# A vision-transformer block in float32: the residual's load is issued one image earlier and moved ahead of the loads of normalised tokens

## The reference

```python
h = _L0_tok_ref(x, L0_tok_W, L0_tok_b)
h = jnp.concatenate([jnp.broadcast_to(cls_tok, (h.shape[0], 1, h.shape[2])), h], axis=1)
h = h + _L0_attn_ref(_layernorm(h, axis=-1), ...)   # softmax(q k' * scale + anchor term) v, times Wo
h = h + _L0_ffn_ref(_layernorm(h, axis=-1), ...)    # round and clip to int8, matmul, scale, bias
return h
```

## Time and profile before

| | |
|---|---|
| median of 3 runs | 1740.1 us (1738.42 to 1743.04) |
| the profiled execution: time, span | 1741.97 us, 1740.2 us |
| attention phase | from about 425 us to the end |
| busy share of the span: PE, DVE, POOL, ACT | 92%, 88%, 61%, 50% |
| length of an odd and an even step together, around 1000 us | about 19.4 us |
| DMA busy share in the attention phase | 0.75 to 0.82 in stretches of 200 us |
| granted TensorE clock in the attention phase | 1.00 of full speed |

### The profile page before, as it was taken

How to read it: one execution, slowest core, us unless ns; L and a number is a source line. 1 busy time by engine, 2 the same in 40 slices (tenths; PEclk the granted TensorE clock), 3 DMA queues, 4 the chain that set the end, 5 groups by cost and what they waited for, 6 DMA issues and landing times.

```text
span 1740.2 us, 52082 instructions
## 1 busy us (share of the span) xinstructions
PE 1607.0 (92%) x15856; PEld 1406.2 (81%) x15856; DVE 1523.9 (88%) x3521; ACT 868.0 (50%) x2008; POOL 1064.6 (61%) x2039
## 2 busy tenths in 40 slices
PE   4999999996699999999999999999999999999995
PEld 4999999995577778888788888878778877878874
DVE  7888888895389899999999999999999999999995
ACT  2000000002266666666666666666666666666663
POOL 3353453535056667676667767676767677676775
PEclk9999999997599999999999999999999999999997
DMA  9998899973677878887888878887888888887851
GB/s 304 273 322 282 316 296 300 323 252 128 113 133 146 147 142 149 145 148 140 143 153 148 146 141 150 145 147 141 147 153 147 144 142 152 145 148 141 148 108 33
DMA packets 216157, 303.64 MB, mean 174 GB/s; under 512 B 47776, under 2 KB 205011, under 8 KB 205988
## 3 DMA queue, kind: packets, MB, share of 16 engines
q1 hardware_dynamic: 204690, 227.17, 66.3%
q10 hardware_dynamic: 7426, 39.47, 7.8%
q0 software_dynamic: 3984, 36.28, 5.4%
HBM read 126.54 MB, written 58.29 MB: 106 GB/s over the span
## 4 chain that ended last, share of the span: by engine, by line
PE 20%; DMA 14%; issue 13%; DVE 13%; SPq 10%; POOL 4%; ACT 2%; DVEq 1%; ACTq 1%; POOLq 0%
DMA h_in<-h_scratch 13%; SPq L766 6%; PE bank L877 5%; DVE neg_max L1184 4%; PE o_bank L933 4%; PE s_pair L911 3%; PE bank L925 2%; DVE x_lo L1248 2%; DVE h L1271 2%; DVE rough L1283 2%; SPq L756 2%; PE bank L898 2%; PE bank L1024 1%; PE bank L1062 1%; SPq L774 1%
## 5 line engine op out<-in xcount | busy, mean ns | idle before, releaser
L1078 ACT ACTIVATE probs<-bank 99x396 f32<-99x396 f32 x768 | 380.3, 495 | 171.9 <-PE bank L925 165.4
L340 PE MATMUL bank<-e_t,xt 128*128 128x192 f32 x2352 | 386.6, 328 | 25.2 <-DVE xt L448 21.5
L340 PEld LDWEIGHTS bank<-e_t,xt 128*128 128x128 f32 x2352 | 385.1, 191 | 26.5 <-DVE xt L448 26.3
L1184 DVE TENSOR_REDUCE neg_max<-s_pair 99x4 f32<-99x788 f32 x384 | 374.1, 974 | 21.1 <-PE s_pair L911 20.9
L1308 POOL TENSOR_TENSOR key_sum<-probs 99x396 f32<-99x396 f32 x256 | 307.8, 1202 | 103.4 <-ACT probs L1078 74.5
L925 PE MATMUL bank<-q_st,k_st 99*99 99x198 f32 x1536 | 297.0, 275 | 5.3 <-ACT probs L1078 4.6
L1346 POOL TENSOR_TENSOR hb<-h,ffn_bias 99x384 f32<-99x384 f32 x128 | 129.1, 1009 | 235.9 <-DVE h L1271 235.9
L925 PEld LDWEIGHTS bank<-q_st,k_st 99*99 99x99 f32 x1536 | 195.8, 166 | 87.6 <-ACT probs L1078 44.5
L911 PE MATMUL s_pair<-k_st,q_st 96*99 96x198 f32 x1536 | 224.4, 269 | 31.7 <-DVE neg_max L1184 30.3
L448 DVE STREAM_TRANSPOSE xt<-x_t 128x256 f32<-128x256 f32 x588 | 215.0, 416 | 43.5 <-PE bank L340 42.1
L933 PE MATMUL o_bank<-probs,vals 99*32 99x198 f32 (+1 forms) x3072 | 224.2, 338 | 0.0
(11 more groups left out here) (137 smaller groups left out, 3703.1 us busy)
## 6 DMA issues: line engine op xcount, KB each, us to landing
x_t<-in_x_dram SPq DMA_DIRECT2D x26, 1344.0 KB, 21.2
x_t<-in_x_dram ACTq DMA_DIRECT2D x26, 1344.0 KB, 22.4
q_st<-qk_hi SPq DMA_DIRECT2D x126, 198.0 KB, 4.3
k_st<-qk_hi SPq DMA_DIRECT2D x126, 198.0 KB, 4.5
xn_in<-xn_scratch SPq DMA_DIRECT2D x128, 148.5 KB
h_in<-h_scratch SPq DMA_DIRECT2D x128, 148.5 KB
h_scratch<-h_t POOLq DMA_DIRECT2D x13, 1344.0 KB, 17.8
xn_scratch<-xn_t POOLq DMA_DIRECT2D x13, 1344.0 KB, 8.1
```

Source lines behind the costliest of these rows:

```text
L340: last = pe.matmul(token_bank(p)[:, 0:D], xt[:, p, c // 3, c % 3, :], e_t[:, row_kind(t), col, c // 3, c % 3, :], start=c == 0, stop=c == 5)
L1078: nc.scalar.activation(probs[:, n.two, h, :, :], wide(T_BANK, TC), ACT.Exp).then_inc(exp_done, 1)
L1184: nc.vector.tensor_reduce(out=neg_max[:, n.two, :, 2 * j:2 * j + 2].rearrange("p c h -> p h c"), in_=both, axis=AX_X, op=ALU.max, negate=T ...
```

## The change

In the step of image i, SP used to issue the residual of image i-2 (`e`), the one that DVE adds in the same step, after the even step's stacks. It now issues the residual of image i-1 (`c`), after the odd step's first two stacks and ahead of `load_xn`. In an even step, which has no stacks at that point, it is the first thing that SP issues. The wait that protects the buffer (`h1_done`, for the image two before) moves with it. Nothing else is changed.

```diff
-                f, p, a, e, k, ahead = i.plus(5), pair_of(i), i.plus(1), i.plus(-2), i.plus(-5), i.plus(7)
+                f, p, a, c, k, ahead = i.plus(5), pair_of(i), i.plus(1), i.plus(-1), i.plus(-5), i.plus(7)
...
                     stack(p, q_st, 0, q_first, qk_hi[:, 0, :])
                     stack(p, q_st, 1, q_first, qk_hi[:, 0, :])
+                if c.within(B):
+                    if c.reuses(NS):
+                        sp.wait_ge(h1_done, c.count(1, 1 - NS))
+                    sp.dma_start(h_in[:, c.two, :, :], h_dram[c.n].rearrange("(c p) d -> p c d", p=TC))\
+                        .then_inc(h_landed[c.slot], 16)
                 if ahead.within(B):
                     load_xn(ahead)
...
                     stack(p, k_st, 1, k_last, qk_lo[:, 2, :])
-                if e.within(B):
-                    if e.reuses(NS):
-                        sp.wait_ge(h1_done, e.count(1, 1 - NS))
-                    sp.dma_start(h_in[:, e.two, :, :], h_dram[e.n].rearrange("(c p) d -> p c d", p=TC))\
-                        .then_inc(h_landed[e.slot], 16)
                 if k.within(B):
```

## The result

The changed kernel takes 1733.96 us (median of 6 runs, 1731.92 to 1739.87) against 1740.2 us before (6 runs). The ratio is 0.9963, with a 95% interval of 0.9948 to 0.9977: faster by about 6 us, where 25 us were forecast, and the time lies inside the stated range of 1703 to 1736 us. The direction was right and the size was not, by a factor of four. A few runs of the whole set were in a slower state (one of e13's six, at 2209.75 us, and three of the kernel before beside e13 to e15), and all ratios leave them out.

What follows compares the result with a forecast made beforehand. A late residual load was taken to stall DVE, and through it PE, once per pair of steps. 28 us regained less 3 us for the stacks gave 25 us: 1715 us against the median, range 1703 to 1736 us.

Steps and rivals of the forecast that it cites:

- The stall that goes: At L1271 DVE no longer waits for the residual; PE gets back its L911 wait for `neg_max`, 28 us.
- What is next at L1271: The output projection is next in line, 0.09 us ahead of DVE, so DVE regains 0.5 of 0.57 us.
- The wait for the buffer: The new load's wait for `h1` of the image two before is met by 0.6 us or more; cost 0.
- The even step, 3 us: Residual ahead of three stacks shifts the last by 0.55 us; mean cost 0.05 us over 61 pairs, 3 us.
- upper bound of 1.1 us: Largest shift of the even step's last stack, if SP's issue and the queue's transfer are both paid.
- the first rival: Shorter odd step makes even-step stacks 1.0 us later; 15 of 28 us given back at L911, 1727 us; chance 0.20.
- The slack: Last stack's landing to the first score's weights: 0.85 us in the typical pair, 0.45 in another, next to nothing in a slow one.
- a pair of 18.9 to 19.1 us: Sign in the profile after: the length of a pair of steps if the forecast is right.
- its second or fourth case: Stacks give part back (0.20) or make it slower (0.08); sign: L911 or `qk_hi` waits for `k_st` of 10 us or more.
- the slower one: Last stack gates every pair before the first score; each 0.3 us longer, 18 us, 1758 us; chance 0.08.
- The odd step, 0 us: The load changes places with two token loads; the same bytes stand before the seven stacks, cost 0.
- The stores, 0: The stores keep their place in both steps, so no cost was put on them.

Runs made afterwards that it cites:

- e13: As e11, with the large load of the normalised tokens cut in two halves too: 1727.8 us, ratio 0.9926.
- e15: Changed kernel with the large load of the normalised tokens, not the residual, cut in two halves: 1719.05 us, ratio 0.988.
- e1: Changed kernel, image ahead kept, but the residual's load issued at its old place behind the even step's three stacks: 1714.95 us, ratio 0.9864.
- e5: Changed kernel with the residual at the new place in odd steps only, at the old place in even steps: 1718.69 us, ratio 0.9875.
- e6: Changed kernel with the residual at the new place in even steps only, at the old place in odd steps: 1725.49 us, ratio 0.9915.
- e10: Changed kernel with the residual's load cut by token chunk into two halves, both at the new place: 1721.19 us, ratio 0.9888.
- e11: As e1, with the residual's load cut by token chunk into two halves, both at the old place: 1706.63 us, ratio 0.9798.
- e3: As e1, with the even step's loads of normalised tokens behind the three stacks too: 1731.08 us, ratio 0.9951.

## Why the prediction was wrong

**The stall that goes: right.** 28 us were to come from PE's wait for `neg_max`. The wait is gone, and where nothing takes its place, in e1, the kernel gains 24 us by its medians (1738.6 to 1714.95).

**What is next at L1271: right.** The output projection, 2.0 us in two waits.

**The wait for the buffer: right.** No wait of SP at L792 appears in the trace after between 500 and 1700 us; SP waits for `mrow_done` and `qkhi_done` as before, for the latter longer (42.8 us against 27.7), which fits ACT's rewriting of `qk_hi` being late.

**The even step, 3 us: the step that failed.** The place, the mechanism and the releaser were right, and the size was nearly eight times too small: 23.5 us of waits at L911 in place of 3, and 19 us of time (the changed kernel against e1). The mis-sized term is the shift of the last stack. The prediction took 0.55 us, since issue and transfer "overlap rather than add". Against SP's row maxima, the measure that it had named itself, the stack now lands 1.11 us later on average: it is issued 0.50 us later and takes 0.60 us longer to land (table above). That is the prediction's upper bound of 1.1 us, but its second half has another source. In e1 the landing is 0.54 us longer too, with the residual behind the stacks. So it is not the transfer of the residual ahead of the stacks. It goes with the shorter odd step, 8.84 us in place of 9.30 from its first stack to the row maxima, which is the 0.46 us that the forecast left out and the first rival put on top. What the place adds is SP's issue time, 0.5 us, near the 0.58 us that the prediction had read as a bound. The idle 0.6 us of the earlier trace rows hid neither.

The slack was read rightly. In the trace before, the time from the last stack's landing to the first score's weights is 0.71 us on average over 61 pairs. By these slacks a shift of 0.55 us in every pair gives 2.2 us of waits, close to the 3 us of the sum, and one of 1.1 us gives 24, close to the 23.5 measured. The second figure is an estimate: the real shift is uneven, and the pair after the loop's turn pays most of it.

The first rival, 1.0 us of shift and 1727 us, was therefore nearest, and the 1733.96 us lie in the band that it was given (1724 to 1735). The time is inside the stated range by that rival and not by the forecast. The signs say the same: the prediction asked for a pair of 18.9 to 19.1 us, and the trace after has 19.52 against 19.58 before, where e1 has 19.11; and it said that 10 us or more of waits for `k_st` would prove its second or fourth case, the first rival or the slower one.

**The odd step, 0 us: wrong.** e5 and e6 put 4 to 8 us on it. The same bytes stand before the seven stacks, but the load now comes before the tokens. How that slows the stacks behind both is open.

**The stores, 0: not contradicted**; nothing was run on them.

**The rule of the Trainium skill** ("DMA: Bandwidth & Descriptors", section "Queues, rings and completion order"), that an increment lands only after the engine's earlier writes, would show here as a longer time from a stack's issue to its landing when the residual is ahead of it. No run shows that apart: 5.92 us in the changed kernel against 5.85 in e1, and 5.14 in e10 against 5.33 in e11. Nor does it cover e3, where 9.3 KB were late through what was issued behind them, or the cut: no run here shows why one DMA of two chunks holds the queue longer than two DMAs of one chunk.

**Still open:** whether it is the number of partitions, the two chunks or the pauses between two issues that makes the cut loads cheaper; why the landing lengthens in the pair after the loop's turn and not in the others as much; and what the bytes ahead would cost if their issue took SP no time.

## What to carry to other kernels

Before a load is moved forward in a queue, find the transfer behind it with the least slack and add up everything that makes it later: the time that the issuing engine needs for the load (0.5 us here), and what goes with the gain of the change itself, here a longer landing (0.5 to 0.6 us). Each alone fits into a slack of 0.7 us in most pairs, and both together do not. Issuing early and issuing ahead are two changes: take the earlier image at the old place first (here 24 us against 6). When a DMA queue is nearly full, the form of a transfer is worth a try by itself, and only together with the wait that it relieves: the same cut gave 8 to 13 us where the stacks were late or nearly so, nothing where DVE's stall set the pace, and a loss of 21 us where one more was added.

## What the runs showed of the hardware that was not expected

The same 148.5 KB over 99 partitions, in two DMAs of 74 KB in place of one, let the 99 KB transfers issued after it land in 2.9 us instead of 3.6 us, and cutting the tokens' load of the same shape did as much for the time. The small transfer of 9.3 KB (`q_st<-max_rows`) was late 39 times, 22.4 us in all, when the large transfers behind it were issued right after it, and 12 times, 4.6 us, when two loads stood between them. A 198 KB transfer within on-chip memory took 5.0 us or 6.97 us to land in neighbouring pairs of the same loop; the long landing recurred in one pair of three (17 of 20 over 6.2 us), with the residual ahead of it or behind it, and went away when a load was cut. And SP's time to issue, about 0.5 us for each load, was itself a price: 4.5 KB and 74 KB ahead of that transfer delayed its issue by the same 0.5 us and its landing after issue not at all (5.39 and 5.29 us, against 5.33 with nothing ahead).
